# The bias b3 as one product of ones inside the last FFN matrix, instead of an addition to x on GpSimd

## The reference

```python
x = x + 0.5 * ffn(layernorm(x))
x = x + attn(layernorm(x))
x = x + 0.5 * ffn(layernorm(x))

def ffn(x):                      # switch_w, switch_b, w1, b1, w2, b2, w3, b3
    gate, top_idx = top_k(softmax(x.reshape(b, -1) @ switch_w.T + switch_b), 2)
    # per batch row two experts of 8, each 32 -> 32 -> 32 on every head of 32 columns
    h = gelu(xh @ w1[top_idx] + b1[top_idx])
    o = (h @ w2[top_idx] + b2[top_idx]) * gate, summed over the two experts
    return (x + o) @ w3.T + b3
```

## Time and profile before

| | |
|---|---|
| median of 3 runs | 664.95 us (662.29 to 667.07) |
| the profiled execution | 664.78 us |
| its span in the trace | 663.1 us |
| mean granted TensorE clock | 0.945 of full |
| TensorE busy | 578.4 us (87%), 2564 products |
| VectorE busy | 464.0 us (70%) |
| ScalarE busy | 227.4 us (34%) |
| GpSimd busy | 143.1 us (22%) |

### The profile page before, as it was taken

One profiled execution on the slowest core, in us unless ns is written; L12 is line 12 of the kernel. 1 busy time (PEld: TensorE's weight loads), 2 busy tenths in 40 slices (PEclk: granted clock), 3 DMA queues, 4 the chain that ended last, 5 costly groups with the idle time before them and its releaser, 6 DMA issues.

```text
span 663.1 us, 7592 instructions
## 1 busy us (share of the span) xinstructions
PE 578.4 (87%) x2564; PEld 427.0 (64%) x2564; DVE 464.0 (70%) x823; ACT 227.4 (34%) x380; POOL 143.1 (22%) x121
## 2 busy tenths in 40 slices
PE   2963868999799999799999979999989946989897
PEld 2862545767567676567666756676667834666676
DVE  4739996776686585677386668546767577898963
ACT  0024753223434232352422343422310055644550
POOL 2135033233001224201223300022321403123000
PEclk9985988999899999999999979999989958999999
DMA  9984040000000100000200000020159230002112
GB/s 364 380 318 156 2 143 0 1 1 0 24 25 21 60 0 1 0 33 16 79 0 0 0 32 16 21 92 1 48 205 385 92 127 1 16 33 95 49 47 80
DMA packets 17132, 49.14 MB, mean 74 GB/s; under 512 B 1616, under 2 KB 1872, under 8 KB 15824
## 3 DMA queue, kind: packets, MB, share of 16 engines
q1 hardware_dynamic: 17104, 48.78, 19.6%
HBM read 40.38 MB, written 8.39 MB: 74 GB/s over the span
## 4 chain that ended last, share of the span: by engine, by line
PE 50%; DVE 25%; issue 12%; ACT 4%; POOL 3%; DMA 3%; SPq 2%; DVEq 0%; ACTq 0%; POOLq 0%
PE bank L566 8%; PE bank L569 8%; PE bank L567 8%; PE bank L337 6%; PE bank L339 5%; PE bank L338 5%; PE bank L442 4%; DVE h_lo L1080 2%; DVE xt L1100 2%; DVE xnw L1063 2%; POOL rs L915 2%; DMA x1p<-in_x 2%; DVE x L1107 2%; DVE xt_lo L1087 2%; ACT hf L729 2%
## 5 line engine op out<-in xcount | busy, mean ns | idle before, releaser
L566 PE MATMUL bank<-xh,win_hi 128*128 128x512 f32 x304 | 131.2, 432 | 0.0
L567 PE MATMUL bank<-xl,win_hi 128*128 128x512 f32 x304 | 120.1, 395 | 0.0
L569 PE MATMUL bank<-xbf,win_lo 128*128 128x512 bf16 x320 | 83.0, 382 | 0.0
L915 POOL TENSOR_TENSOR rs<-ms,neg_half 128x16 f32<-128x16 f32 x16 | 46.8, 2926 | 140.6 <-ACT ms L794 140.6
L566 PEld LDWEIGHTS bank<-xh,win_hi 128*128 128x128 f32 x304 | 57.8, 190 | 15.1
L567 PEld LDWEIGHTS bank<-xl,win_hi 128*128 128x128 f32 x304 | 57.7, 190 | 11.3
L337 PE MATMUL bank<-w_hi,z_hi 128*128 128x512 f32 x128 | 51.7, 404 | 7.0 <-DVE x L1107 6.6
L729 ACT ACTIVATE hf<-bank,w_sel 128x512 f32<-128x512 f32 x64 | 42.0, 689 | 35.0 <-PE bank L339 24.0
L569 PEld LDWEIGHTS bank<-xbf,win_lo 128*128 128x128 bf16 x320 | 24.8, 98 | 40.6 <-issue 21.8
L902 POOL TENSOR_TENSOR xa<-xa,b_half 128x512 f32<-128x512 f32 x28 | 38.0, 1382 | 58.9 <-DVE xnw L1063 58.9
L339 PE MATMUL bank<-w_hi,z_lo 128*128 128x512 f32 x128 | 50.1, 391 | 0.0
(11 more groups left out here) (155 smaller groups left out, 1202.4 us busy)
## 6 DMA issues: line engine op xcount, KB each, us to landing
route_w<-in_switch_w SPq DMA_DIRECT2D x4, 2048.0 KB, 10.5
route_w<-in_switch_w SPq DMA_DIRECT2D x16, 512.0 KB, 12.7
xa<-in_x SPq DMA_DIRECT2D x6, 1024.0 KB, 5.8
raw<-in_w_in SPq DMA_DIRECT2D x4, 1280.0 KB, 5.4
out<-x SPq DMA_DIRECT2D x16, 256.0 KB, 2.0
x_dram<-x1p SPq DMA_DIRECT2D x12, 256.0 KB, 2.0
xa<-x_dram SPq DMA_DIRECT2D x3, 1024.0 KB, 5.7
x1p<-in_x SPq DMA_DIRECT2D x2, 1024.0 KB, 8.0
```

The lines of the kernel that those rows point to most:

```text
L566: pe.matmul(bank[:], win_hi[:, c, r, k, :], xh[:, k, :], start=(k == 0), stop=False)
L567: pe.matmul(bank[:], win_hi[:, c, r, k, :], xl[:, k, :], start=False, stop=False)
L569: mm = pe.matmul(bank[:], win_lo[:, c, r, k, :], xbf[:, k, :], start=False, stop=(k == KC - 1))
L915: pool.tensor_tensor(rs[:], ms[:], neg_half[:], ALU.pow).then_inc(s_rs, 1)
```

## The change

b3 is loaded to 64 partitions in a free piece of the tile raw and halved by ScalarE as before. GpSimd then multiplies rows 0 to 31 by column 0 of the identity, and rows 32 to 63 by its column 32, so that of each 32 rows only the first keeps 0.5 b3 and the others are zero. A copy to fp32r rounds all 64 rows (high part), and in rows 32 to 63 the subtraction raw - rounded leaves the low part. A product of ones (64 x 128) by these 64 rows puts high plus low part of 0.5 b3 into every token row of the bank. It opens each W tile. The 32 additions on GpSimd and the semaphore s_xb are gone.

```diff
-        ones = sb("ones", [P, P])
+        ones_r = sb("ones_r", [P, P], F32R)
+        ones = ones_r[:].bitcast(F32)
...
-        b3_half = sb("b3_half", [P, D])
+        b3_rows = sb("b3_rows", [2 * HD, D], F32R)
...
+        b3_raw = raw[0:2 * HD, 1, KC * D:]
...
-                sp.dma_start(b3_half[:], b3.partition_broadcast(P)).then_inc(s_small, 16)
+                sp.dma_start(b3_raw, b3.partition_broadcast(2 * HD)).then_inc(s_small, 16)
...
                 bank_free(job)
-                project(t, bank, use["z_hi"], use["z_lo"], w3_hi, w3_lo, chunk_wait=z_ready)
+                pe.wait_ge(s_b3l, 1)
+                pe.matmul(bank[:], ones_r[0:2 * HD, :], b3_rows[:], start=True, stop=False)
+                project(t, bank, use["z_hi"], use["z_lo"], w3_hi, w3_lo, chunk_wait=z_ready, begun=True)
...
-            act.activation(b3_half[:], b3_half[:], ACT.Copy, scale=0.5).then_inc(s_b3, 1)
+            act.activation(b3_raw, b3_raw, ACT.Copy, scale=0.5).then_inc(s_b3r, 1)
...
-            pool.wait_ge(s_b3, 1)
-            for t in range(NT):
-                residual_bias(0, t)
+            pool.wait_ge(s_b3r, 1)
+            pool.wait_ge(s_rp, NT)
+            for row in (0, HD):
+                part_of = slice(row, row + HD)
+                own.do(pool.tensor_tensor(b3_raw[part_of], b3_raw[part_of],
+                                          ident[part_of, row:row + 1].to_broadcast([HD, D]), ALU.mult))
+            own.do(pool.tensor_copy(b3_rows[:], b3_raw))
+            pool.tensor_tensor(b3_rows[HD:2 * HD], b3_raw[HD:2 * HD], b3_rows[HD:2 * HD],
+                               ALU.subtract).then_inc(s_b3l, 1)
+            pool.wait_ge(s_b3l, 1)
...
                 for c in range(KC):
                     group(b, c)
-                    if c == 2:
-                        residual_bias(b + 1, 0)
-                        residual_bias(b + 1, 1)
-                residual_bias(b + 1, 2)
-                residual_bias(b + 1, 3)
                 ln_rstd(b + 1)
...
-            for f in range(B, 2 * B):
-                for c in range(KC):
-                    residual_bias(f, c)
...
-                ve.wait_ge(s_xb, NT * f + t + 1)
                 ve.wait_ge(s_ob, job + 1)
```

More of the change, by code:

```diff
@@ L240, in macaron_kernel @@
         s_pc = sem("s_pc")
-        s_b3 = sem("s_b3")
+        s_b3r = sem("s_b3r")
+        s_b3l = sem("s_b3l")
         s_w3h = sem("s_w3h")
@@ L257, in macaron_kernel @@
         s_xn = sem("s_xn")
-        s_xb = sem("s_xb")
         s_t1 = sem("s_t1")
@@ L502, in experts_out, with project @@
                 mm.then_inc(s_ob, 1)
-            def project(t, bank, a_hi, a_lo, w_hi, w_lo, chunks=range(KC), chunk_wait=lambda k: None):
+            def project(t, bank, a_hi, a_lo, w_hi, w_lo, chunks=range(KC), chunk_wait=lambda k: None, begun=False):
                 tok = slice(t * P, (t + 1) * P)
@@ L509, in project @@
                     mm = mm3(pe, bank[:], a_hi[:, k, tok], a_lo[:, k, tok], w_hi[:, k, :], w_lo[:, k, :],
-                             k == 0, k == KC - 1)
+                             k == 0 and not begun, k == KC - 1)
                 if chunks[-1] == KC - 1:
@@ L896, in route_rstd @@
                                    ALU.pow).then_inc(s_rp, 1)
[L898 to L902, removed]
             def ln_rstd(b):
```

## The result

The changed kernel takes 667.09 us (median of 20 runs, 665.69 to 668.37), the kernel before 665.11 (20 runs): ratio 1.0029, interval 1.0015 to 1.0043. It is 2.0 us slower; 662.0 was forecast, a gain of 2.8 against the profiled execution. The time is inside the range of the forecast, but the change made the kernel slower and not faster. The page of the profile shows what moved in the large: TensorE holds 61% of the chain that ended last where it held 50%, VectorE 17% where it held 25%.

The account below looks back on a forecast made before the run. The chain of waits was half TensorE, a quarter VectorE, which GpSimd's additions slowed. Start 0, first block +0.7, loop +1.2, block 4 -1.75, blocks 5 and 6 -4.6, block 7 +1.6: -2.85, so 662.0 us, range 656.5 to 669.0.

Parts of the forecast that it names:

- What bounds: Whole kernel: TensorE bounds the W phases of the first block and loop; in the last phase TensorE waits for late VectorE.
- I take 0.23, as its type, width and bank are those of its neighbours.: Each W tile: the added b3 product costs 0.23 us, with 30 of 32 on the path.
- The high end of my bounds: Each W tile: at most 0.50 us per added product, the record of one that starts behind a wait.
- the first rival: W tiles: TensorE can't overlap the small products; loads exposed on both sides give 673 us, on one 667.7; chance 0.10 together.
- The removed additions: GpSimd's 32 additions of b3 gone: VectorE is no longer slowed in the loop, block 4, blocks 5 and 6 and start.
- The waits: Blocks 5 and 6: TensorE's waits of 1.76 and 0.31 us for W drains go whole; some 0.3 of the 1.15 stays.
- The new work at the start: Start: GpSimd's four new operations meet the first normalisation as the old additions did; counted 0, from -1.8 to +0.5 us.
- The loop: Three loop rows: each gains 0.51 us on y_lo and pays 0.92 for four products; +0.41 a row, +1.2 us together.
- Rounds 5 and 6: Last phase, blocks 5 and 6: TensorE gains some 3.2 us a round and pays 0.92; -2.3 each, -4.6 us together.
- The late waits stay: Last phase: some other link holds the W drains, so gains of 1.75 and 6.4 us don't come; 670.1 us, chance 0.10.
- The clock: Long TensorE waits: fewer slow-clock stretches of 1.7 us each, with the first normalisation free besides; 655.7 us, chance 0.15.

## Why the prediction was wrong, point by point

- **What bounds.** Right: TensorE alone in the W phases, VectorE's lateness in the last phase. Both showed as described.
- **"I take 0.23, as its type, width and bank are those of its neighbours."** This step failed. The product costs 0.66 in line. The high end of my bounds, 0.50, was the length of a record, which is not a price in line, and so didn't even hold the truth: the gap behind the product was missing from it. The products cost 14.6 us instead of 6.9. It was the first rival, an exposed load on each side, priced 0.188 each or 0.38 for both; measured 0.43 for both. That the row count brings it is shown (128 rows, two in a row, 32 rows); how the 0.43 divides between the loads and an idle array isn't. I gave the rival 0.10. Its price, 673, took every one of 30 products as fully on the path, over a gain that I had too small.
- **Why the argument for 0.23 was no argument.** Loads hidden between 128-row products said nothing on a change of row count, and I knew that no row shows one. The Trainium skill, TensorE: Matmul & The Clock Gate, Part 3, says that a load overlaps a running matmul only when the row groups differ. The 64-row product shares its rows with its neighbours and its load is exposed: there the trace agrees (0.43 us). Two 128-row products share all their rows and the load of 0.188 us is hidden, as they start 0.23 apart: there it disagrees, in every run. What the runs show is that the load hides where the row count stays the same, and I had let the second fact outweigh the first case, which it doesn't touch.
- **The removed additions.** Direction and places right, sum too small: 11.5 us in my terms (1.8 of them at the start), 15.2 measured. In the last phase 3.5 a round instead of 3.2, and 1.65 ahead of it instead of 1.75. The waits did what I forecast: 1.76 and 0.31 went whole, and of the 1.15 there stays 0.34 in the run without additions. They are 2.88 of the 3.53; the other 0.65 are the slower starts behind waits, for which I had taken some 0.3. The start gives 2.4 instead of 1.8, the clock included.
- **The new work at the start.** I counted 0 against the old additions; the kernel with it and without product or additions is 2.3 slower than the one without it (1.65 of it before the first drain, 84.14 to 82.49), and the old additions cost 2.4 there. Right, as far as the clock at the start lets it be seen. The normalisation takes 3.31 us where I said near 3.8.
- **The loop.** Forecast +0.4 a row. The y_lo gain came (0.51), the products took 2.0 in the W phase between first and last drain alone, and 0.66 ahead of it: some 2.1 longer a row instead of 0.4.
- **Rounds 5 and 6.** Forecast 2.3 shorter each, measured 3.2 and 2.2: right for partly wrong reasons, as the additions had cost more and the products were dearer. With 128 rows a round takes 25.3 to 25.4 against 25.2 without product: there the product is nearly free.
- **The late waits stay** (rival, 0.10). Refuted: none of 0.3 us or more is left in the rounds of the changed kernel.
- **The clock** (rival, 0.15). It came in part, and it hid some of the loss. The mean granted clock was 0.953 to 0.961 in all runs of the changed kernel; of the 24 runs of the kernel before timed beside the experiments, 22 had 0.943 to 0.949. The two that had 0.956 took 661.68 and 661.81 us, the eight of the changed kernel with 0.956 took 666.70 to 667.92. At that clock the change costs some 5 us and not 2. The additions are the side from which it comes: without them the mean was 0.952 to 0.960. The kernel before at 0.956 and the one without additions at 0.955 and 0.957 (650.61 and 649.56) are 11.6 us apart, close to the 11.5 of my terms, so most of what 15.2 has over them goes with the clock. A mean over a whole run is a rough measure, and no experiment held the clock fixed.
- **The sum of it.** -12.9 for all but the product where -9.75 was forecast, +14.6 for the product where +6.9 was forecast. The first error took 3.2 us off the second, 7.7; that the time fell inside the range is luck. With a product that costs what the forecast priced (128 rows), the kernel gains 1.06%, where the forecast had 0.4%: the direction comes back, and the size is still off.

What stays open: how much of the unassigned 1.7 us of the additions is the clock and how much work, what in the change of row count keeps the load from starting early, and whether the price differs for 96 rows or for a small product whose rows lie in other partitions than 0 to 63. Behind transposes the three steps are 0.20, 0.43 and 0.34 with 64 rows, and 0.03, 0.32 and 0.23 with 128: 0.39 more, near the 0.41 in the stream of W products.

## What to carry to other kernels

A small product inside a stream of full ones wasn't priced by its columns here: where the row count of the stationary operand changed, two weight loads came out from under the stream (0.43 us). Pad it with zero rows to its neighbours' shape, or put several small ones in a row. And when a price has no row in the trace, the bound must include what the neighbours lose, not only what the instruction takes. What GpSimd takes from VectorE is dear only where VectorE holds the chain, and is found there by the longest record of a line beside its median.

## What the runs showed of the hardware

- A product of 64 or 32 rows between products of 128 rows costs 0.66 us by the tile where a 128-row product costs 0.23 by its step and 0.28 by the tile (3.00 after 2.72); the extra 0.43 is paid once for two small products in a row.
- A GpSimd operation stretches tensor_scalar and a subtraction with two SBUF inputs on VectorE: 3.89 us for four tensor_scalar and 3.46 for two h_lo beside additions, 1.91 and 1.29 without. In the last phase before, the stretched ones end 0.3 to 0.6 us behind the addition beside which they started. An addition with one input from a PSUM bank (xt, at 553.11 before, beside four GpSimd additions from 549.95 to 555.57) took 0.74, its mean over the program.
- GpSimd's operations are priced by columns, not by partitions: a 32-row product of 512 columns takes 1.03 us, a 32-row subtraction 1.32, a 64-row copy 0.69, beside a 128-row product of 1.06 and a 128-row addition of 1.38.
